# Post-norm decoder, second cross-attention: output projections and norms a unit later and tile by tile, both score pairs first, the fourth maximum behind the weighted sums

## The reference

```python
x = _layernorm(x + _L0_attn_ref(...)); x = _layernorm(x + _L0_xattn_ref(...)); x = _layernorm(x + _L0_ffn_ref(...))
x = _layernorm(x + _L1_attn_ref(...))
x = _layernorm(x + _L1_xattn_ref(ctx_1024, ctx_1024, x, ...))      # the stage changed
x = _layernorm(x + _L1_ffn_ref(...))

def _L1_xattn_ref(values, keys, query, Wv, Wk, Wq, Wo, bo):
    v, k, q = each reshaped to (N, L, 16, 16) and multiplied by its 16x16 matrix
    energy = einsum('nqhd,nkhd->nhqk', q, k)
    attention = softmax(energy / sqrt(256), axis=-1)
    out = einsum('nhql,nlhd->nqhd', attention, v).reshape(N, Lq, 256)
    return out @ Wo.T + bo

def _layernorm(x, eps=1e-5):
    return (x - mean(x)) / sqrt(var(x) + eps)
```

## Time and profile before

| | |
|---|---|
| median of 3 runs | 2830.38 us (2827.75 to 2834.51) |
| profiled execution | 2816.93 us, span 2815.0 us |
| mean granted clock of TensorE | 0.952 |
| busy: PE, DVE, ACT, POOL | 2569.0, 1468.7, 1128.8, 1086.5 us |
| the stage changed | from about 1960 to 2470 us of the span |
| its units with a full load | 26.1 us (odd) and 27.3 us (even) |

### The profile page before, as it was taken

How to read it: one execution, slowest core, us unless ns; L and a number is a source line. 1 busy time by engine, 2 the same in 40 slices (tenths; PEclk the granted TensorE clock), 3 DMA queues, 4 the chain that set the end, 5 groups by cost and what they waited for, 6 DMA issues and landing times.

```text
span 2815.0 us, 36748 instructions
## 1 busy us (share of the span) xinstructions
PE 2569.0 (91%) x13798; PEld 1529.8 (54%) x13798; DVE 1468.7 (52%) x3205; ACT 1128.8 (40%) x1614; POOL 1086.5 (39%) x735
## 2 busy tenths in 40 slices
PE   5786999999999999997999999687999999889997
PEld 3343556565556555654556665455333333368886
DVE  3444555555555555554433333366677777455455
ACT  3544344444444444442122222132576767631111
POOL 4665466666765676563100000142323323110001
PEclk8997999999999999997899999889799999999999
DMA  2001100000000000003899999510000000000000
GB/s 104 9 9 34 36 12 24 21 19 12 27 18 20 12 12 25 12 1 115 346 372 380 388 386 378 193 39 18 16 22 18 21 17 10 13 16 21 23 23 32
DMA packets 60322, 229.21 MB, mean 81 GB/s; under 512 B 16601, under 2 KB 30577, under 8 KB 44273
## 3 DMA queue, kind: packets, MB, share of 16 engines
q1 hardware_dynamic: 54256, 209.27, 20.2%
q0 software_dynamic: 3584, 9.84, 1.2%
q10 hardware_dynamic: 2304, 7.75, 0.7%
HBM read 216.73 MB, written 9.70 MB: 80 GB/s over the span
## 4 chain that ended last, share of the span: by engine, by line
PE 76%; DVE 9%; issue 4%; DMA 4%; ACT 3%; POOL 3%; SPq 1%; POOLq 0%; ACTq 0%; DVEq 0%
PE PS L680 8%; PE PS L1488 7%; PE PS L663 6%; PE PS L2087 6%; PE PS L711 5%; PE PS L721 4%; PE PS L1506 4%; PE PS L1110 4%; PE PS L2075 4%; PE PS L1125 3%; DMA m_fb<-in_m_fb 3%; PE PS L695 3%; PE PS L1143 3%; DVE y_Mx L1247 2%; PE PS L744 2%
## 5 line engine op out<-in xcount | busy, mean ns | idle before, releaser
L944 POOL TENSOR_TENSOR x_A<-x_A,x_P 128x1024 f32<-128x1024 f32 x190 | 451.4, 2376 | 203.1 <-ACT x_P L791 189.1
L871 DVE CUSTOM_DVE_ANT_0 x_junk<-PS,x_mb 128x512 bf16<-128x512 f32 x512 | 331.0, 685 | 352.2 <-PE PS L695 351.9
L1247 DVE TENSOR_REDUCE y_Mx<-PS 128x1 f32<-128x512 f32 x512 | 324.4, 685 | 126.6 <-PE PS L1143 126.6
L791 ACT ACTIVATE x_P<-PS,x_kb 128x1024 f32<-128x1024 f32 x256 | 271.8, 1112 | 222.8 <-PE PS L667 218.3
L1197 ACT ACTIVATE y_P<-PS 128x1024 f32<-128x1024 f32 x256 | 255.0, 1023 | 113.8 <-PE PS L1125 109.8
L1488 PE MATMUL PS<-m_w,m_xt 128*128 128x512 f32 x624 | 282.8, 596 | 0.6 <-issue 0.6
L680 PE MATMUL PS<-x_P,x_V 128*64 128x512 f32 x1024 | 248.8, 607 | 0.0
L663 PE MATMUL PS<-x_Q,x_K 64*128 64x512 f32 x1536 | 228.4, 400 | 0.0
L1143 PE MATMUL PS<-y_K,y_Q 16*128 16x512 f32 x512 | 188.2, 515 | 32.5 <-DVE y_Mx L1247 28.8
L2087 PE MATMUL PS<-n_xp,n_wp 128*128 128x512 f32 x816 | 211.8, 409 | 4.3 <-POOL n_wp L2203 4.3
L1709 POOL DMA_INDIRECT m_xb<-xd,m_idxi x39 | 37.1, 951 | 405.1 <-PE PS L1476 372.7
(11 more groups left out here) (333 smaller groups left out, 4239.8 us busy)
## 6 DMA issues: line engine op xcount, KB each, us to landing
m_w<-in_m_w SPq DMA_DIRECT2D x39, 2048.0 KB, 11.0
m_fb<-in_m_fb SPq DMA_DIRECT2D x39, 1024.0 KB, 12.9
m_v<-in_m_w SPq DMA_DIRECT2D x39, 1024.0 KB
x_w<-in_x_w SPq DMA_DIRECT2D x32, 384.0 KB, 3.0
ys<-m_yb SPq DMA_DIRECT2D x39, 128.0 KB
n_wg<-in_n_w SPq DMA_DIRECT2D x17, 256.0 KB, 2.8
x_cT<-in_ctxT SPq DMA_DIRECT2D x4, 1024.0 KB, 5.2
y_c<-in_ctxT SPq DMA_DIRECT2D x6, 512.0 KB, 3.7
```

Source lines behind the costliest of these rows:

```text
L791: act.e.activation(Pt[gt % 6][:], PS[:, 2 * i:2 * i + 2, :], ACT.Exp, bias=kb[u // 8 % 2][:, kt:kt + 1], scale=scale).then_inc(s["exp"], 1)
L871: dve.e.tensor_tensor_reduce(junk[j % 2][:], ring.bank("max", v, j), mb[b % 2][:, half * 512:half * 512 + 512], 1.0, -3e38, ALU.add, ALU.m ...
L944: pool.e.tensor_tensor(A[u % 2][:], Pt[(gt - 1) % 6][:] if kt == 1 else A[u % 2][:], Pt[gt % 6][:], ALU.add).then_inc(s["add"], 1)
L1247: dve.e.tensor_reduce(Mx[v % 2][:, h, qt, half:half + 1], ring.bank("max", v, j), AX.X, ALU.max).then_inc(s["red"], 1)
```

## The change

The new order of a window is: first scores, a, b, second scores, c, side work, weighted sums, d, then the rest. In window 5 "mq" stands ahead of it all. The output projection of a finished batch moves one unit on (windows 3 to 6 of the second unit after), one tile a window, each with its residual, statistics and, in the unit after that, its scaling. No arithmetic is added or taken away.

```diff
+        def dve_scale(dve, j, b, i):
+            dve.wait_ge(ln["rstd"], j + 1)
+            dve.e.tensor_scalar(x[:, 4 * b + i, :], x[:, 4 * b + i, :], mv[:, i, 0:1], rstd[:, i:i + 1],
+                                ALU.subtract, ALU.mult).then_inc(ln["nrm"], 1)
...
-                6: [("pv", 0, 6), ("wo", -1, 0), ("res", -1, 0), ("wo", -1, 1)],
...
-            at = {t: [("sc", 0, 0), *maxima(t)[:2], *([("mq", 1, 0)] if t == 5 else []), *[w for w in between[t] if w[0] not in ("pv", "ev")],
-                      ("sc", 0, 1), *maxima(t)[2:], *[w for w in between[t] if w[0] in ("pv", "ev")], *after[t]] for t in range(T)}
...
+            beside = {0: [("k", 2, 0)], 1: [("k", 2, 1)], 2: [("q", 2, 0)], 3: [("v", 2, 0), ("wo", -2, 0)], 4: [("v", 2, 1), ("wo", -2, 1)],
...
+            at = {t: [*([("mq", 1, 0)] if t == 5 else []), ("sc", 0, 0), *maxima(t)[:2], ("sc", 0, 1), *maxima(t)[2:3], *beside[t],
+                      ("pv", 0, t), *maxima(t)[3:], *behind[t]] for t in range(T)}
...
                         elif name == "st":
-                            dve.wait_ge(s["res"], 4 * (b + 1))
-                            dve_stats(dve, 20 + b, b)
+                            dve.wait_ge(s["res"], 4 * b + j + 1)
+                            dve_stat(dve, 20 + b, b, j)
                         elif name == "nr":
-                            dve_norm(dve, 20 + b, b)
+                            dve_scale(dve, 20 + b, b, j)
...
-                        elif name == "st":
+                        elif name == "st" and j == 3:
                             pool_rstd(pool, 20 + v // 4)
```

More of the change, by code:

```diff
@@ L1025, in maxima @@
                 return [("max", 2 if t > 4 else 1, j + i) for i in range(4)]
[L1026 to L1032, removed]
-                6: [("pv", 0, 6), ("wo", -1, 0), ("res", -1, 0), ("wo", -1, 1)],
[L1034 to L1037, removed]
-            at = {t: [("sc", 0, 0), *maxima(t)[:2], *([("mq", 1, 0)] if t == 5 else []), *[w for w in between[t] if w[0] not in ("pv", "ev")],
-                      ("sc", 0, 1), *maxima(t)[2:], *[w for w in between[t] if w[0] in ("pv", "ev")], *after[t]] for t in range(T)}
+            beside = {0: [("k", 2, 0)], 1: [("k", 2, 1)], 2: [("q", 2, 0)], 3: [("v", 2, 0), ("wo", -2, 0)], 4: [("v", 2, 1), ("wo", -2, 1)],
+                      5: [("wo", -2, 2)], 6: [("wo", -2, 3)], 7: []}
+            behind = {0: [("ev", -1, 0), ("xb", 0, 0)], 1: [("nr", -3, 0)], 2: [("nr", -3, 1)], 3: [("rec", -1, 0), ("res", -2, 0), ("nr", -3, 2)],
+                      4: [("res", -2, 1), ("st", -2, 0), ("nr", -3, 3), ("tp", -3, 0)],
+                      5: [("turn", 1, 0), ("mul", -1, 0), ("res", -2, 2), ("st", -2, 1)],
+                      6: [("res", -2, 3), ("st", -2, 2), ("tp", -3, 1)], 7: [("st", -2, 3)]}
+            at = {t: [*([("mq", 1, 0)] if t == 5 else []), ("sc", 0, 0), *maxima(t)[:2], ("sc", 0, 1), *maxima(t)[2:3], *beside[t],
+                      ("pv", 0, t), *maxima(t)[3:], *behind[t]] for t in range(T)}
             def windows():
```

## The result

The changed kernel takes 2847.39 us, the median of 20 runs (2835.18 to 2868.55), against 2831.99 us for the kernel before (20 runs, 2816.86 to 2852.20): ratio 1.0056, 95% interval 1.0035 to 1.0077. It is slower by 15.4 us; 9.7 had been forecast.

The account below looks back on a forecast made before the run. TensorE, busy 91%, sets the time, idling for VectorE's reductions. Windows +5.0 and batch ends +4.7 make +9.7 us on the profiled 2816.93, 2826.6; with 13.45 to the median, 2840. Range 2827 to 2857.

Parts of the forecast that it names:

- two loops through the ring: The ring's three banks close one loop in plain windows, a longer one in side windows; +6 to +17 us, 58%.
- The steps of the loops: Distances read from the old timeline: 0.56 for d, 0.60 between reductions, 0.75 to free a bank, 1.05 projection, 0.99 sums.
- Part 1, the loop through d: Windows without side work: d, its reduction, c', sums, d' take 2.73 us against 2.98; 47 windows, -11.8 us.
- Part 2, side work behind a' behind d: Windows with side work: it waits for the bank of a', reduced after d; 3.95 us against 3.58; 56 windows, +20.7.
- Part 3, window 5: Window 5, transposes now behind d beside VectorE's loop: 3.1 us against 3.51, a gain of 0.4; 14 windows, -5.6.
- The reciprocal: Window 3's reciprocal behind d's reduction, side window following in seven even units: 0.24 each, +1.7 us.
- the steady part: Plain, side and fifth windows plus the reciprocal, without batch ends: sum +5.0 us.
- Part 4, the end of a batch: Tile-by-tile output projection in windows 3 to 6: 14.6 us a batch, 12.4 in the third; together 41.6, +4.7.
- The clock: Rival: one dip of 1.26 us in each of 15 units, +19 on top, 2859 us; 8%.
- the 0.5 level in plain units: Sign of being wrong: the granted clock shows its 0.5 level in plain units.
- The other 13.45 us: Distance from the profiled execution to the median of runs before, added unchanged to 2826.6, giving 2840 us.
- The copies of the row maxima: Sign of being wrong: these DMA copies, with two shorter windows, arrive late at a unit's first scores; no size given.

Follow-up runs that it names:

- four first: Changed kernel with the fourth maximum put ahead of the side work and the weighted sums, nothing behind the sums; 2842.95 us in one run.
- end of batch only: Changed kernel with the old order within a window, only the end of a batch moved and cut into tiles; 2811.66 us, 0.9960 of before.
- paired: Changed kernel reordered: windows 0 to 4 start a, side work, b, both scores; 5 to 7 start a, both scores, b, c; 2868.48 us, 1.0161 of before.
- crossed-then-paired: Paired's order from unit 6 on; up to unit 5 another order (windows 1 to 4: a, first scores, b, side work, second scores); 2782.94 us, 0.9829 of before.
- side-between-a-and-b: Changed kernel with side work between a and b, small work ahead of the weighted sums, d last; 2911.15 us, 1.0237 of before.

## Why the prediction was right, and where it was not

The direction, the range and the mechanism (two loops through the ring) hold. The sum of 9.7 fell short of the 15.4 between the medians, and of the 30.6 between the two traces, because the clock at the ends of batches had been put at nothing.

- *The steps of the loops*: 0.56 had been taken from d to the start of its reduction, 0.53 came. The end at 2106.52, from which the prediction reads VectorE's 0.06, is that of a row of scores (2106.11 + 0.41) and not of a maximum; it did little harm. The projection was to start 1.6 behind the first scores; it starts 1.88 behind them, as the prediction's own terms give (0.56 + 0.60 + 0.75).
- *Part 1, the loop through d*: 2.73 said, 2.70 measured, and shortened to 2.43 when d's reduction was halved but not when a's was. 47 windows x -0.28 = -13.2 (-11.8 said).
- *Part 2, side work behind a' behind d*: 3.95 said, 3.93 measured. 56 x 0.35 = +19.6 (+20.7 said).
- *Part 3, window 5*: 3.1 was said and 3.65 came, but the window behind it was 2.21 instead of 2.73; together 5.86 against 5.83. The sum of this part is right, its place was not.
- *The reciprocal*: 0.24 a piece was said; windows 4 of even units are 4.07 against 3.96 in window 3, so 0.11. With the small work ahead of d they are 3.96.
- Together the steady part is +3.5 (+5.0 said), read from whole units: seven pairs at 28.47 + 25.70 against 27.35 + 26.12, and five windows of unit 14 at -0.28. With a clock of 1.00 throughout it would hardly be measurable.
- *Part 4, the end of a batch*, is the term that was mis-sized. What an end adds was to grow from 12.1 to 14.6; it is (40.35 - 25.70) + (33.39 - 28.47) = 19.6 at the first batch, 19.5 at the second. The part without the clock holds in sum: 4.79 in window 3 (4.75 said), 5.53 in window 4 of unit 13, at a clock of 1.00 (5.35 said), 4.86 in window 6 (5.61 said, too high), while window 5 is about 6.7 (8.34 less the 1.6 of its "wo"; 5.61 said, too low). The low clock cost 7.17 - 5.53 = 1.6 in window 4 of unit 5, 1.6 in window 5 and some 2.2 in window 0 of unit 6 (6.41, against 4.19 at 1.00 in the kernels with half a reduction). Without these 5.4 the end of a batch is 14.2 by this estimate, against 14.6 said. The third end was worst, since unit 14 took 31.55 us.
- *The move of the end of a batch* was not priced apart from the loops. Alone, in the old order of windows, it is a gain: (33.97 - 26.12) + (28.52 - 27.35) = 9.0 for what an end adds, 3.1 less than before, at a clock of 1.00.
- *The clock* was a rival at 8%, thought of as a dip in every plain unit. No plain unit had one by itself, but units 4 and 8, which follow the late DMAs, were at 0.94: the 0.5 level in plain units and late copies had both been named as signs of being wrong, and both showed. The dips came at the ends of batches, where TensorE waits 0.64 to 0.76 us for a residual and soon again for a reduction, and after the late DMA below; and in unit 14 the low clock stayed (0.51 over 27.37 us, windows of 4.16 instead of 2.70). The section of the Trainium skill that was weighed ("TensorE: Matmul & The Clock Gate", "A second HAM failure mode: psum-queue depth-cycling") was set aside on the evidence of the plain windows. For those it stays set aside, and four first, with its waits of mostly 0.57 at a clock of 1.00 throughout, speaks against it too. At the ends of batches the trace agrees with it, at clocks of 0.92 and 0.90. Which waits lower the clock is open: no run varied one wait by itself, and "end of batch only" has one of 0.75 for a residual, in unit 5, without a dip.
- *The other 13.45 us*: the forecast put the same distance between profile and median on both kernels. It was 15.1 for before (2831.99 - 2816.93) and -0.1 for after. That the forecast of the median came near (2840 for 2847.39) is in part luck: this error (13.5 too much) and the missing clock cost cancelled.
- *The copies of the row maxima*, named as a sign of being wrong, did arrive late at the first scores of two units. In unit 7 the last of the four DMAs was issued by 2233.49, and the first scores of unit 8 started 2.35 us later, after a wait (its releaser is not marked; "issue" stands there. These scores wait only for the copies, for GpSimd's "lo" and for ScalarE's exponentials, and the last two were over, so the copies are inferred):

```profile
2231.05 2.44 SPq L1331 DMA_DIRECT2D y_Q<-y_NM  x4
```
```profile
2235.84 0.50 PE L1125 MATMUL PS<-y_Q,y_K 32*128 32x512 f32 x2 [0.72 <-issue]
```

That made window 7 of unit 7 3.91 instead of 2.73, and of unit 3 3.65; a dip of the clock followed each. In the kernel before the same place of unit 7 is 3.48 instead of 2.98. Why these copies take longer just there was not found.

## What to carry to other kernels

When a piece of work is moved so that its own wait vanishes, ask which piece next takes the buffer that it frees, in ring order, and add up that loop; here one maximum moved behind 1 us of other work shortened the plain windows by 0.28, and side work moved behind c lengthened the others by 0.35. Fill a wait with work that does not itself need the buffer that is waited for, and put small work of the releasing engine where that engine is idle, not between two reductions on the loop. Look at the granted clock before believing a sum of windows: a kernel whose order leaves TensorE no gap lost 46 us by starting at the low clock and keeping it for 260 us, and the same order from unit 6 on, behind one that had raised the clock, was part of a kernel 47 us faster than before.

## What the runs showed of the hardware

- TensorE can be busy 43.60 of 43.60 us and stay at 1.2 GHz for 260 us (paired), and the same order of instructions stays at 2.4 GHz once there (units 6 to 13 of crossed-then-paired). It left 1.2 GHz with the first output projection tile (2225.74 to 2229.10). So the clock in this stage depends on its past as well as on the work. All runs of paired (2866.58 to 2872.24) agree with a low start, those of side-between-a-and-b vary by 86 us.
- Two maxima on the rows of heads that are not being scored cost next to nothing beside the scores: the group takes 0.67, four scores alone 0.66 (2433.80 to 2434.46 in the kernel before, unit 14). With one of them on the rows of a head that is being scored, the group takes 0.90.
